# One adaLN transformer kernel: its second layer run over three turns instead of two, and its 32x32 turns moved from TensorE to VectorE and DRAM

## The chip, the cores and the metric

One Trainium2 chip, one of its cores. The metric is the device time in microseconds (us) of one execution of the whole program. The engines are TensorE (PE, with its weight loads as PEld), VectorE (DVE), ScalarE (ACT), GpSimd (POOL) and SyncE (SP), which issues most transfers. All data are float32.

## The reference, cut to what matters

Eight sequences of 512 tokens with 256 features pass through a layer 0, then through layer 1, whose attention block is itself a stack of four pre-norm blocks, then through a grouped attention with a mixture of experts. The change touches the stack of four blocks only:

```
for i in range(4):
    x = x + self_attention(layer_norm(x, ln1_g[i], ln1_b[i]), Wq[i], Wk[i], Wv[i], Wo[i], bo[i])
    h = layer_norm(x, ln2_g[i], ln2_b[i])
    x = x + (gelu(h @ W1[i] + b1[i], approximate=False) @ W2[i] + b2[i])
```

Of the 8 heads of 32 features, 4 are local: a block of 128 queries sees its own and the preceding block of keys through a masked softmax. The other 4 are linear: softmax over the features of q, elu(k) + 1, running sums of k^T v over buckets of 64 tokens. W1 is 256x1024, W2 is 1024x256.

## The kernel before, in words

The function `layer1` holds this stack. A sequence in a block is one **turn** g, and there are 4 x 8 = 32 turns, numbered 0 to 31, always in the order block by block and sequence by sequence; the residual rows of all sequences stay in the tile `y`. Each engine has its own hand-written list, and semaphores with counts that grow with g tie them together. The PE list has 33 rounds: in round g it does the attention of turn g and the MLP (`hidden`, the product with W1, then `down`, the product with W2) of turn g - 1, cut into pieces between the attention's steps. There are two PSUM banks `M[0]` and `M[1]` (6 and 7) for the MLP, two `V` banks (4 and 5) and four `S` banks (0 to 3) for attention.

A round on PE before the change: `project` (tokens' values, then q and k, L1408 and L1415), `turn` (eight 128x128 transposes of the normed rows `xn` against the identity, L1398, whose result ScalarE scales into `h2T`), `scores` (L1425), eight `hidden` products (L1435) with the linear heads' `linear_turn` (L1442), `scores` of query blocks 2 and 3 and `context` (L1449) in between, `linear_out` (L1461), then 32 `down` products (L1473) in four pieces with `probs_turn` behind each (L1489: 28 transposes of the probabilities), `values` (L1501), `out_proj` (L1516).

On the other engines, in the order of their lists: VectorE adds the attention's result to `y` (`attn_sum`, L1190), takes mean and variance (`stats`, L1137, L1140) and norms (`norm`, L1146) for the second layer norm, prepares the linear heads (L1202 to L1212), masks the scores and takes their minimum (L1222), sums the contexts (`context_sum`, L1229 to L1239), inverts the sums of exponentials (`invert`, L1245), norms the next turn's rows, copies the turned probabilities out of PSUM (`probs_out`, L1251) and adds the MLP's result (`mlp_sum`, L1197). ScalarE copies PSUM to SBUF, takes exponentials (`exps`, L1336) and Gelu (L1373), with a table load at each change of function. GpSimd takes the inverse deviation (L1070, L1071), adds the biases (L1105, L1118), scales the linear queries (L1109) and multiplies the probabilities with the inverted sums (`normalise`, L1090).

The first layer norm's rows of turns 1 to 31 already go another way, `move_turned1`: one VectorE instruction transposes `xn` in blocks of 32x32 (L1154) into `score`, SyncE writes the blocks with four transfers of 128 KB into DRAM (L1013), waits until they have landed, and reads them back as 512 KB with the features on the partitions (L1017). SyncE's list is in order: a wait in it holds back every transfer behind it. It also loads weights at a block's first and last sequences and, in 8 turns, writes 1 MB of zeros each for a later stage (L1002).

In rounds 0 to 6 and 26 to 31 VectorE and GpSimd also norm and modulate a sequence on its way into or out of the stack (`stats_x`, `modulate`, `gated`). `idle_products` are products that nobody reads; they stand where PE has no MLP to do.

## Time and profile before

| what | value |
|---|---|
| median of 3 runs | 3123.52 us (3122.75 to 3123.99) |
| the profiled execution's own time | 3120.52 us |
| its span, first to last instruction | 3118.7 us |
| mean granted TensorE clock | 0.979 |
| PE busy | 2921.5 us (94%) |
| DVE, ACT, POOL busy | 1676.6, 1415.3, 827.9 us |
| layer 1's 32 turns and the end of its MLP | from 717.85 to 2477.52 us of the span |

In the profile a line L1435 is line 1435 of the kernel. A group's row tells the engine, the line, the operation, what it writes and reads, how often, its busy time in total and the mean length of one; matmuls overlap, so that a matmul's own length is more than its share of the time. A timeline row tells start, length, engine and line of instructions in a row; in brackets stands the idle time before it and who ended it. A float32 matmul stands in the trace as two records. A row of the windows view tells the stretch, its length, then busy time and instructions of PE, PEld, DVE, ACT and POOL, the granted clock of PE (1.00 is full speed), the busy share of the transfer engines and what they moved in GB/s.

### The profile page before, as it was taken

What the parts mean: (1) busy time and instruction counts of PE and PEld (TensorE: products, weight loads), DVE (VectorE), ACT (ScalarE), POOL (GpSimd) and SP (SyncE); (2) the same over time, 40 slices, a digit from 0 to 9 for tenths busy, and PEclk for the clock granted to TensorE, in tenths of its full rate; (3) what the DMA queues carried; (4) which work ended last, traced back from release to release, by engine and by line L of the source; (5) the groups of instructions that cost most, each with busy time, mean ns of one, the idle gap of its engine ahead of it and who ended that gap; (6) DMA issues with size and microseconds to landing.
All of it is one profiled execution on the core that took longest, in us unless ns stands there. A gap on an engine that the chain in (4) does not pass through costs nothing. (4 is left out here: it accounts for less than half of the span.)

```text
span 3118.7 us, 53260 instructions
## 1 busy us (share of the span) xinstructions
PE 2921.5 (94%) x20742; PEld 1958.5 (63%) x20742; DVE 1676.6 (54%) x5013; ACT 1415.3 (45%) x3117; POOL 827.9 (27%) x829
## 2 busy tenths in 40 slices
PE   6889999888999999999999999999999788799998
PEld 3566666664666666565666666665656444468887
DVE  4677776755655545545445444456555478641112
ACT  3666666633445354444444453544444134132224
POOL 1001111113323322322323223233333310025552
PEclk8999999999999999999999999999999899899999
DMA  4111111002000112010211000110100000023325
GB/s 140 18 19 19 18 19 19 13 3 72 25 28 18 38 31 69 28 55 28 67 47 35 21 14 28 32 55 20 38 20 25 11 1 28 27 68 80 75 84 189
DMA packets 102249, 126.48 MB, mean 41 GB/s; under 512 B 12451, under 2 KB 79014, under 8 KB 100960
## 3 DMA queue, kind: packets, MB, share of 16 engines
q1 hardware_dynamic: 93168, 102.56, 11.4%
q0 software_dynamic: 7680, 16.32, 2.1%
q8 instruction: 166, 2.72, 0.4%
q10 hardware_dynamic: 1152, 4.19, 0.3%
q14 instruction: 83, 0.68, 0.1%
HBM read 75.56 MB, written 43.61 MB: 38 GB/s over the span
## 5 line engine op out<-in xcount | busy, mean ns | idle before, releaser
L1435 PE MATMUL bank<-h2T,w 128*128 128x512 f32 x1024 | 478.8, 606 | 5.2 <-ACT gT L1373 3.7
L1473 PE MATMUL bank<-w,gT 128*128 128x256 f32 x2048 | 465.9, 381 | 0.0
L1473 PEld LDWEIGHTS bank<-w,gT 128*128 128x128 f32 x2048 | 379.3, 190 | 49.7 <-issue 0.5
L1090 POOL TENSOR_TENSOR prob<-prob,rsum 128x512 f32<-128x512 f32 (+1 forms) x256 | 237.9, 950 | 592.4 <-DVE rsum L1245 592.4
L1435 PEld LDWEIGHTS bank<-h2T,w 128*128 128x128 f32 x1024 | 182.2, 190 | 223.8 <-issue 173.6
L1373 ACT ACTIVATE gT<-bank,vec 128x512 f32<-128x512 f32 x256 | 175.1, 687 | 285.5 <-PE bank L1435 284.0
L609 ACT ACTIVATE y<-y,least 128x128 f32<-128x128 f32 (+3 forms) x512 | 252.0, 554 | 50.6 <-DVE least L479 50.6
L479 DVE CUSTOM_DVE_ANT_0 y<-bank,mask 128x128 f32<-128x128 f32 (+3 forms) x512 | 223.9, 485 | 70.2 <-PE bank L706 68.9
L1222 DVE CUSTOM_DVE_ANT_0 prob<-bank,mask 128x256 f32<-128x256 f32 (+1 forms) x512 | 164.3, 387 | 168.3 <-PE bank L1425 168.3
L1336 ACT ACTIVATE prob<-prob,least 128x256 f32<-128x256 f32 (+1 forms) x512 | 239.6, 471 | 15.8 <-DVE least L1222 15.5
L1251 DVE COPY probT<-bank 128x1024 f32<-128x1024 f32 (+1 forms) x128 | 138.4, 1082 | 189.7 <-PE bank L1489 189.7
L722 PE MATMUL bank<-ident,y 128*128 128x128 f32 x1280 | 183.5, 280 | 46.3 <-DVE probT L284 33.3
L1408 PE MATMUL bank<-wtok,hT 128*128 128x512 f32 x512 | 225.0, 592 | 1.3 <-ACT hT L1327 1.3
L722 PEld LDWEIGHTS bank<-ident,y 128*128 128x128 f32 x1280 | 143.5, 142 | 110.8 <-issue 90.0
L1390 ACT COPY aoT<-bank 128x512 f32<-128x512 f32 x32 | 18.8, 586 | 366.6 <-PE bank L1501 366.6
L1354 ACT COPY tok<-bank 128x384 f32<-128x384 f32 x128 | 61.3, 479 | 234.9 <-PE bank L1408 234.9
L1408 PEld LDWEIGHTS bank<-wtok,hT 128*128 128x128 f32 x512 | 97.2, 190 | 110.2 <-issue 108.6
L2371 DVE COPY yout<-bank 128x512 f32<-128x512 f32 x40 | 27.7, 692 | 256.8 <-PE bank L2503 256.8
L284 DVE COPY probT<-bank 128x512 f32<-128x512 f32 (+1 forms) x160 | 101.2, 633 | 119.1 <-PE bank L722 119.1
L1146 DVE TENSOR_SCALAR xn<-y,mv,rstd 128x256 f32<-128x256 f32 x256 | 132.9, 581 | 52.3 <-POOL rstd L1071 52.3
L2491 PE MATMUL bank<-inT,we 128*128 128x256 f32 x640 | 144.8, 379 | 2.4 <-ACT inT L2422 2.4
L2503 PE MATMUL bank<-we,score 128*128 128x256 f32 x640 | 144.6, 379 | 0.0
(328 smaller groups left out, 5050.2 us busy)
## 6 DMA issues: line engine op xcount, KB each, us to landing
turned_rows<-score SPq DMA_DIRECT2D x124, 128.0 KB, 2.3
score<-turned_rows SPq DMA_DIRECT2D x31, 512.0 KB, 3.6
w<-in_W SPq DMA_DIRECT2D x8, 1024.0 KB, 7.6
expert_parts<-zeros SPq DMA_DIRECT2D x8, 1024.0 KB, 6.1
we<-in_we SPq DMA_DIRECT2D x16, 512.0 KB, 5.0
rows<-modulation SPq DMA_DIRECT2D x40, 128.0 KB, 3.5
x<-in_x SPq DMA_DIRECT2D x8, 512.0 KB, 6.3
prob<-score SPq DMA_DIRECT2D x64, 64.0 KB, 2.3
```

The source lines that it names most:

```text
L479: nc.vector.tensor_tensor_reduce(out=prob[:, j, FROM[tile]:FROM[tile] + width], in0=S[:, j, at:at + width], in1=mask[:, T - width:T], scal ...
L609: ins = nc.scalar.activation(one, one, ACT.Exp, bias=least[:, n % 2, tile, j:j + 1], scale=-1.0)
L722: ins = nc.tensor.transpose(H[at % 2][:, col:col + P], prob[:, j0 + j, src:src + P], c.ident[:, :])
L1090: nc.gpsimd.tensor_tensor(two, two, rsum[:, at:at + 2].unsqueeze(2).to_broadcast([P, 2, width]), ALU.mult).then_inc(s["probs"], 1)
L1222: nc.vector.tensor_tensor_reduce(out=prob[:, at, from_col(q):PAIR], in0=S[:, j, off:off + width], in1=mask[:, from_col(q):PAIR], scale=1.0 ...
L1336: nc.scalar.activation(one, one, ACT.Exp, bias=least[:, at:at + 1], scale=-1.0, accum_out=sums[:, at:at + 1]).then_inc(s["exped"], 1)
L1373: nc.scalar.activation(gT[:, m, :], M[m % 2][:, :], ACT.Gelu, bias=v[:, 4 * KD + m:4 * KD + m + 1]).then_inc(s["gelu_done"], 1)
L1408: ins = nc.tensor.matmul(S[:, t, :], hT[:, k, 1 + t * P:1 + (t + 1) * P], wtok[:, k, :], start=(k == 0), stop=(k == KD - 1))
L1435: ins = nc.tensor.matmul(M[m % 2][:, :], w1[:, k, m * P:(m + 1) * P], h2T[:, k, :], start=(k == 0), stop=(k == KD - 1))
L1473: ins = nc.tensor.matmul(M[i][:, (t % 2) * D:(t % 2 + 1) * D], gT[:, m, t * P:(t + 1) * P], w2[:, m, :], start=(m == 0), stop=(m == MF - 1))
L2491: ins = nc.tensor.matmul(UP[(2 * j + i) % 4][:, (m % 2) * CHUNK_T:(m % 2 + 1) * CHUNK_T], w1[e % 2][:, k, m * P:(m + 1) * P], inT[j % 2][: ...
L2503: ins = nc.tensor.matmul(DOWN[j % 2][:, t * D:(t + 1) * D], gT[j % 2][:, k, t * P:(t + 1) * P], w2[e % 2][:, k, :], start=(k == 0), stop=( ...
```

## The change

- The MLP of a turn is spread over two later rounds: round g does `hidden` of turn g - 1 and `down` of turn g - 2, so that there are 34 rounds. `down` now stands in the first half of a round, `hidden` in the second. `down` waits for all eight Gelus of its turn.
- `turn` for the second layer norm is gone from the rounds: `turn_rows` transposes both norms' rows in 32x32 blocks on VectorE, `move_rows1` and `move_rows2` take them through DRAM, and ScalarE's `gains_in` scales both.
- `probs_turn` and `probs_out` are gone: `turn_probs` transposes the probabilities in 32x32 blocks from `prob` to a new tile `prob_blocks` on VectorE, and `move_probs` takes them through DRAM in two halves: query blocks 0 and 1 (12 blocks of 32 columns, 768 KB), then 2 and 3 (16, 1 MB), each as four transfers out, a wait, and one back in. `values` waits for each half.
- Seven of eight `hidden` products stand ahead of `values`, one behind it (`EARLY`).
- GpSimd's bias `bo` is added earlier, and the first norm of the next turn moves to the end of VectorE's list. The zeros are written in 32 pieces of 256 KB, two in each of 16 turns.

```diff
-            for g in range(TURNS + 1):
-                mlp, attn = g > 0, g < TURNS
+            for g in range(TURNS + 2):
+                attn, down_of, hidden_of = g < TURNS, g >= 2, 1 <= g <= TURNS
                 if attn:
                     project(g)
-                if mlp:
-                    pe.wait_ge(s["norm2"], g)
-                    for half in range(KD):
-                        if g >= 2:
-                            pe.wait_ge(s["w2_added"], 2 * (g - 2) + half + 1)
-                        turn(half, "turn2_full")
+                if down_of:
+                    down(g - 2, 0, 4)
                 if attn:
                     pe.wait_ge(s["lin_out"], g + 1)
                     pe.wait_ge(s["qk_out"], 2 * (g + 1))
                     scores(g, (0, 1))
-                if mlp:
-                    pe.wait_ge(s["w1_loaded"], 16 * ((g - 1) // B + 1))
-                for m in range(MF):
-                    if mlp:
-                        hidden(g - 1, m)
-                    if attn:
-                        if m == 0:
-                            linear_turn(g)
-                        if m == 2:
-                            pe.wait_ge(s["score_min"], 16 * g + 8)
-                            scores(g, (2, 3))
-                        if m == 3:
-                            pe.wait_ge(s["lin_k_ready"], g + 1)
-                            context(g)
-                if mlp:
-                    pe.wait_ge(s["w2_loaded"], 16 * ((g - 1) // B + 1))
+                if down_of:
+                    down(g - 2, 4, 12)
+                elif attn:
+                    idle_products(c, 4, 7)
+                if attn:
+                    pe.wait_ge(s["score_min"], 16 * g + 8)
+                    scores(g, (2, 3))
+                if down_of:
+                    down(g - 2, 12, 17)
+                if attn:
+                    linear_turn(g)
+                    pe.wait_ge(s["lin_k_ready"], g + 1)
+                    context(g)
+                if down_of:
+                    down(g - 2, 17, NT * MF)
+                elif attn:
+                    idle_products(c, 4, 7)
                 if attn:
                     pe.wait_ge(s["qlT_out"], g + 1)
-                    if not mlp:
-                        idle_products(c, 7, 7)
                     linear_out(g)
-                pieces = NT * MF
-                at = 0
-                for q, upto in enumerate((10, 17, 24, pieces)):
-                    if mlp:
-                        down(g - 1, at, upto)
-                        at = upto
-                    elif q in (1, 2):
-                        idle_products(c, 1, 7)
-                    if attn:
-                        probs_turn(g, q)
+                if hidden_of:
+                    pe.wait_ge(s["w1_loaded"], 16 * ((g - 1) // B + 1))
+                    for m in range(EARLY):
+                        hidden(g - 1, m)
+                elif attn:
+                    idle_products(c, 7, 7)
                 if attn:
                     values(g)
+                if hidden_of:
+                    for m in range(EARLY, MF):
+                        hidden(g - 1, m)
+                if attn:
                     out_proj(g)
```

```diff
+            def move_probs(g, h):
+                sp.wait_ge(s["probs_turned"], 4 * g + 2 * h + 2)
+                if g:
+                    probs_in[h].wait(sp, 16 * g)
+                    sp.wait_ge(s["av_full"], g)
+                dram = c.probs_dram[h]
                 for i in range(GROUPS):
...
+                    src = pblocks[h][SQUARE * i:SQUARE * (i + 1), :, :, :].rearrange("p a k r -> p a (k r)")
+                    sp.dma_start(dram[:, :, i, :].rearrange("a p n -> p a n"), src).then_inc(probs_away[h].sem, 16)
+                probs_away[h].wait(sp, 16 * GROUPS * (g + 1))
+                sp.dma_start(probT[h].rearrange("p i k r -> p (i k r)"), dram.rearrange("a p i n -> (a p) (i n)"))\
+                  .then_inc(probs_in[h].sem, 16)
...
-            for g in range(TURNS):
+            for g in range(TURNS + 2):
...
+                if 1 <= g <= TURNS:
+                    move_rows2(g - 1)
...
+                if g < TURNS:
+                    move_probs(g, 0)
+                    move_probs(g, 1)
...
+                if g + 1 < TURNS:
+                    move_rows1(g + 1)
+                if B <= g < B + parts // 2:
+                    clear(2 * (g - B))
+                    clear(2 * (g - B) + 1)
```

```diff
                     context_sum(g)
-                    invert(g, 0)
+                    turn_probs(g, 0)
+                    invert(g, 2)
+                    turn_probs(g, 1)
+                    if g >= 2:
+                        mlp_sum(g - 2, 0)
+                    invert(g, 3)
+                    if g >= 2:
+                        mlp_sum(g - 2, 1)
+                    turn_probs(g, 2)
+                    turn_probs(g, 3)
```

The order of the instructions at the three places on which the prediction rests:

PE, from the context to the output projection of one turn in the middle of the stack, before (`h2T,w` is `hidden`, `w,gT` is `down`, `ident,prob` the probabilities' transposes, `probT,tok` is `values`, `wo,aoT` is `out_proj`):

```order
L1449 MATMUL bank<-v_linear,tok 32x33 x28
L1435 MATMUL bank<-h2T,w 128x512 x8
L1461 MATMUL bank<-qlT,ctx_normed 32x64 x28
L1473 MATMUL bank<-w,gT 128x256 x10
L1489 MATMUL bank<-ident,prob 128x128 x4
L1473 MATMUL bank<-w,gT 128x256 x7
L1489 MATMUL bank<-ident,prob 128x128 x8
L1473 MATMUL bank<-w,gT 128x256 x7
L1489 MATMUL bank<-ident,prob 128x128 x8
L1473 MATMUL bank<-w,gT 128x256 x8
L1489 MATMUL bank<-ident,prob 128x128 x8
L1501 MATMUL bank<-probT,tok 32x128 x28
```

and the same engine after the change, one whole turn from the second half of `down`'s first piece on:

```order
L1534 MATMUL bank<-w,gT 128x256 x8
L1485 MATMUL bank<-kT,qT 128x256 x8
L1534 MATMUL bank<-w,gT 128x256 x5
L1504 MATMUL bank<-ident,tok 128x128 x4
L1511 MATMUL bank<-v_linear,tok 32x33 x28
L1534 MATMUL bank<-w,gT 128x256 x15
L1523 MATMUL bank<-qlT,ctx_normed 32x64 x28
L1497 MATMUL bank<-h2T,w 128x512 x14
L1547 MATMUL bank<-probT,tok 32x128 x28
L1497 MATMUL bank<-h2T,w 128x512 x2
L1562 MATMUL bank<-wo,aoT 128x256 x8
```

The 28 transposes between the pieces of `down` are gone, `down` stands ahead of the linear heads' output, and 14 of 16 `hidden` matmuls stand between that and `values`.

VectorE, from the contexts' last instruction to the last sum of the MLP, before:

```order
L1239 TENSOR_TENSOR ctx_normed<-ctx,kcum 128x224
L1245 RECIPROCAL rsum<-sums 128x4
L1137 BN_STATS bn<-y 128x6 x4
L1140 BN_AGGR mv<-bn 128x2 x4
L1245 RECIPROCAL rsum<-sums 128x4
L1146 TENSOR_SCALAR xn<-y,mv,rstd 128x256 x4
L1154 STREAM_TRANSPOSE score<-xn 128x4x8x32
L1251 COPY probT<-bank 128x512
L1245 RECIPROCAL rsum<-sums 128x4
L1251 COPY probT<-bank 128x1024
L1197 TENSOR_TENSOR y<-y,bank 128x512
```

and after, to the transpose of the next turn's rows:

```order
L1297 TENSOR_TENSOR ctx_normed<-ctx,kcum 128x224
L1213 STREAM_TRANSPOSE prob_blocks<-prob 128x4x4x32
L1303 RECIPROCAL rsum<-sums 128x4
L1213 STREAM_TRANSPOSE prob_blocks<-prob 128x8x4x32
L1255 TENSOR_TENSOR y<-y,bank 128x512
L1303 RECIPROCAL rsum<-sums 128x4
L1255 TENSOR_TENSOR y<-y,bank 128x512
L1213 STREAM_TRANSPOSE prob_blocks<-prob 128x8x4x32 x2
L1183 BN_STATS bn<-y 128x6 x4
L1186 BN_AGGR mv<-bn 128x2 x4
L1192 TENSOR_SCALAR xn<-y,mv,rstd 128x256 x4
L1198 STREAM_TRANSPOSE score<-xn 128x4x8x32
```

The four copies of turned probabilities have become four transposes, the last two of them behind both sums of the MLP (L1255), and the norm of the next turn's rows stands behind them.

SyncE, one turn in which zeros are written, before:

```order
L1013 DMA turned_rows<-score 32x8x128 x4
L1017 DMA score<-turned_rows 128x2x512
L1002 DMA expert_parts<-zeros 128x2048
```

and after:

```order
L1028 DMA turned_rows<-score 32x8x128 x4
L1030 DMA score<-turned_rows 128x2x512
L1057 DMA turned_probs<-prob_blocks 32x4x384 x4
L1059 DMA probT<-turned_probs 128x1536
L1057 DMA turned_probs<-prob_blocks 32x4x512 x4
L1059 DMA probT<-turned_probs 128x2048
L1028 DMA turned_rows<-score 32x8x128 x4
L1030 DMA score<-turned_rows 128x2x512
L1020 DMA expert_parts<-zeros 128x512 x2
```

Five transfers of a turn have become twenty, in one queue: second norm, first half of the probabilities, second half, first norm of the next turn.

## Rows read from the trace of the kernel before

**Rows 1.** The windows view: turn 0, turns 2 to 25, turns 26 to 31, the end, one stretch

```profile
717.85:761.97 44.12, 37.42 (x291) 20.78 (x292) 25.61 (x83) 15.19 (x46) 13.46 (x14) 0.88 0.11 32
815.57:2100.31 1284.74, 1279.54 (x9025) 819.39 (x9024) 652.82 (x2048) 590.44 (x1392) 392.92 (x371) 1.00 0.12 36
2100.31:2429.47 329.16, 321.19 (x2257) 204.17 (x2255) 187.08 (x581) 145.58 (x346) 116.20 (x106) 1.00 0.08 24
2429.47:2477.52 48.05, 30.77 (x105) 20.08 (x104) 17.84 (x49) 8.34 (x11) 9.37 (x9) 0.85 0.00 0
752.70:756.10 3.40, 3.12 (x13) 2.15 (x12) 1.22 (x1) 0.00 (x0) 2.30 (x3) 0.51 0.45 115
```

**Rows 2.** The timeline of PE in the turn that starts at 1511.67 us

```profile
1521.97 1.04 PE L1398 MATMUL bank<-ident,xn 128*128 128x128 f32 x8
1522.94 0.94 PE L1425 MATMUL bank<-kT,qT 32*128 32x128 f32 x16
...
1534.27 7.13 PE L1435 MATMUL bank<-h2T,w 128*128 128x512 f32 x16
1541.33 0.98 PE L1461 MATMUL bank<-qlT,ctx_normed 32*32 32x64 f32 x56
...
1546.66 0.60 PE L1489 MATMUL bank<-ident,prob 128*128 128x128 f32 x4
1547.10 3.19 PE L1473 MATMUL bank<-w,gT 128*128 128x256 f32 x14
```

**Rows 3.** The timeline of DVE in the same turn

```profile
1515.96 1.38 DVE L1146 TENSOR_SCALAR xn<-y,mv,rstd 128x256 f32<-128x256 f32 x4 [1.54 <-POOL rstd L1071]
...
1548.49 1.25 DVE L1154 STREAM_TRANSPOSE score<-xn 128x1024 f32<-128x1024 f32 x1
...
1552.34 0.68 DVE L1197 TENSOR_TENSOR y<-y,bank 128x512 f32<-128x512 f32 x1
```

**Rows 4.** Groups of instructions by line over the whole span, for ACT, POOL and PE

```profile
L1336 ACT ACTIVATE prob<-prob,least 128x256 f32<-128x256 f32 (+1 forms) x512 | 239.6, 471 | 15.8 <-DVE least L1222 15.5
L1090 POOL TENSOR_TENSOR prob<-prob,rsum 128x512 f32<-128x512 f32 (+1 forms) x256 | 237.9, 950 | 592.4 <-DVE rsum L1245 592.4
L1343 ACT ACTIVATE hT<-score,vec 128x512 f32<-128x512 f32 x62 | 47.2, 813 | 0.0
L1516 PE MATMUL bank<-wo,aoT 128*128 128x256 f32 x512 | 127.6, 392 | 2.4
L1501 PE MATMUL bank<-probT,tok 128*32 128x128 f32 x1792 | 62.2, 276 | 2.8
```

**Rows 5.** The timeline of the transfers' issues on SP, two turns

```profile
1549.77 1.84 SPq L1013 DMA_DIRECT2D turned_rows<-score  x4
1553.47 0.38 SPq L1017 DMA_DIRECT2D score<-turned_rows  x1
...
1335.71 1.84 SPq L1013 DMA_DIRECT2D turned_rows<-score  x4
1341.27 0.38 SPq L1017 DMA_DIRECT2D score<-turned_rows  x1
```

**Rows 6.** The page's DMA issues: KB each, median us from issue to landing

```profile
score<-turned_rows SPq DMA_DIRECT2D x31, 512.0 KB, 3.6
w<-in_W SPq DMA_DIRECT2D x8, 1024.0 KB, 7.6
expert_parts<-zeros SPq DMA_DIRECT2D x8, 1024.0 KB, 6.1
```

**Rows 7.** The timeline of PE: an idle gap in turn 0, then the end of the stack

```profile
752.16 0.63 PE L1489 MATMUL bank<-ident,prob 128*128 128x128 f32 x4 [2.42 <-POOL prob L1090]
...
2435.12 1.97 PE L1398 MATMUL bank<-ident,xn 128*128 128x128 f32 x8 [5.49 <-DVE xn L1146]
2437.19 14.83 PE L1435 MATMUL bank<-h2T,w 128*128 128x512 f32 x32
2451.86 13.98 PE L1473 MATMUL bank<-w,gT 128*128 128x256 f32 x64
```

284 lines of the change are left out of this document (147 added, 137 removed).

## The prediction, on record before the changed kernel ran

> **What bounds the kernel now.** I read the windows view first. Turns 2 to 25 take 1284.74 us, so 53.53 us each, PE is busy for 1279.54 us of that, and the granted clock is 1.00 [rows 1]. In this stretch nothing but PE's own work counts: a microsecond taken from PE's list is won, one taken from another engine is not, until that engine becomes late. Turns 26 to 31 take 54.86 us each (329.16 / 6), because VectorE also serves sequences that leave the stack. Turn 0 (44.12 us) and the end behind the last output projection (48.05 us) are the places where PE waits, with clocks of 0.88 and 0.85. VectorE is busy for half of a middle turn (652.82 of 1284.74 us), ScalarE for 46%. So the question is twofold: how much PE work goes, and does anything that replaces it arrive later than PE gets there?
>
> **What goes from PE.** The timeline of one turn [rows 2] gives each piece from start to start. The eight transposes of the normed rows take 1521.97 to 1522.94, 0.97 us. Four transposes of probabilities take 1546.66 to 1547.10, 0.44 us, so the 28 of a turn 3.08 us. Together 4.05 us of 53.53; nothing of them was hidden, since PE has no gaps. The other products are the same in number and shape; only their place changes. The turned probabilities that `values` now reads lie in runs of 32 floats, not in one of 128; no row shows such a read on PE, and I take it at nothing (upper bound: as much as `values` itself again, 62.2 / 32 = 1.9 us a turn [rows 4]). A middle turn becomes **49.5 us**.
>
> **What is added, and its cover.** VectorE: four copies out of PSUM go, four transposes of the same sizes come, which by the existing transpose cost 1.25 us each and half for the narrow one [rows 3], together 4.4 us. One more transpose of rows, 1.25 us, is new. Even with nothing taken off for the copies VectorE has 27.2 + 5.6 = 33 us of work in 49.5, so its total is no issue, its order is. ScalarE scales `h2T` from SBUF instead of PSUM, the same two instructions. GpSimd does the same work in another order.
>
> The transfers are what can be late. The row pattern is known: four writes of 128 KB are issued at 1549.77, landed by 1553.47 (3.70 us for 512 KB), and the read back of 512 KB lands 3.6 us later [rows 5, 6]. The worst write set before took 5.56 us (1335.71 to 1341.27) [rows 5].
>
> For the second half of the probabilities, 1 MB each way, the rows give bounds. A read of 512 KB takes 3.6 us; 1 MB of zeros, issued 0.4 us behind such a read, takes 6.1 us [rows 6]. So 1.5 MB land in about 6.5 us: 2.9 us for each added MB, and 5.0 us for 1 MB alone. The write set gets 3.70 + 0.5 x 2.9 = 5.15 us as long as its pieces are no more efficient; they are 2 KB long instead of 512 bytes, so I take 4.5. Sum **9.5 us**, between 8.7 (what two 512 KB legs and 0.7 us a leg give) and 12.6 (5.56 and a weight-like read of 7 us).
>
> **Does it arrive?** PE has, from the end of `down` to the second half of `values`: `linear_out` 0.9 us (1541.33 on), seven `hidden` products at 7.07 / 4 = 1.77 us [rows 2], 12.4 us, and the first 12 of 28 products of `values`, 0.8 us: 14.1 us. VectorE, from the same moment: the second sum of the MLP, 0.7 us, two transposes, 2.5 us [rows 3], so 3.3 us with the hand-overs. That leaves **10.8 us** for 9.5 us of transfers: it arrives with about 1.3 us to spare. The probabilities of the last query block must be scaled by then. On ScalarE they stand behind the copy of `qlT` (0.6), one set of four exponentials (4 x 0.47 = 1.9), the two gains (2 x 0.81) and the last set (1.9), 6.0 us from the end of `linear_turn` [rows 4]; then GpSimd needs 2 x 0.95 = 1.9 us. PE fills the same time with the context and 15 `down` products at 13.98 / 32 = 0.44 us [rows 7], 6.6 us and more. So they are ready a good microsecond after `down` ends at the latest, before the 2 us at which VectorE asks for them. The first half starts 5 us earlier and is no issue.
>
> The second norm's rows: attention's sums, statistics and norm end 5.6 us into the turn (at the end of the stack the same chain takes 2429.47 to 2435.12 [rows 1, 7]), the transpose 1.25 and two legs 7.3 bring them in at 14.3 us. ScalarE asks for them after some 22 us and PE at 29 us: hidden. The next turn's rows: on VectorE statistics, inverse deviation and norm (that 5.6 us without the sum, 4.7) and a transpose, 1.25, behind the 3.3 us, then 7.3 us of transfers and 1.6 us of gains, 18 us after `down` ends; PE's next `project` comes after 0.9 + 8 x 1.77 + 1.9 + 4.0 = 21 us [rows 4]. Hidden with 3 us in hand, and SyncE, where they stand behind the second half's write set only (its read is issued, not awaited), is free by then. The weight loads of the three block changes share the engines with a read; at 1 us each they cost 3 us at most, and I leave them in the range.
>
> In ten of the turns 2 to 31 VectorE has 5 us more to do (`stats_x`, `modulate`), now ahead of `context_sum`. It had some 4 us of slack there, so the last transposes come up to a microsecond later and eat the 1.3 us. Such turns cost between nothing and the 1.35 us that the last six show now (54.86 - 53.51). I take 0.5 us, 5 us in all.
>
> **Head.** Turn 0 has no cover: its last probabilities are ready near 31 us (now 35, with the norm of the next rows ahead of them), then transpose and legs 9.5, the last part of `values` 1.2, a copy 0.6, `out_proj` 4.0: 47 us, and a slow stretch of clock, 1 us: 48. Turn 1 loses its `down` (14 us of PE work) and is bound by the same chain: 47. Together 95 for 97.7 now: -3 us.
>
> **End.** Now: norm at 5.65, `hidden` 14.83, `down` 13.98 [rows 7], and 11.7 us to the next stage (2465.8 to 2477.5): 48.05. After: `down` of turn 30 runs first, 14 us; the sums that free its banks stand on VectorE behind a sequence's `stats_x` and `modulate` and end near 19 us (the rows through DRAM are in at 16 us); `hidden` 15, the last Gelu 0.8, `down` 14, then 11.7: 60.5. **+12.5 us.** The pipeline's extra depth costs no more than this, since the `down` of turn 30 is work that turn 31 no longer does.
>
> **Sum.** Turns 2 to 31: now 1284.74 + 329.16 = 1613.9 us; after 30 x 49.48 + 5 = 1489.4: -124.5. Head -3, end +12.5: **-115 us**. The profiled execution took 3120.5 us, its span 3118.7, so it becomes 3005.5. The median of the runs shown is 3.0 us above it: **3008 us**.
>
> **The page's rule against it.** What the rows show is that two small legs through DRAM cost 7.3 us for 512 KB that a strided pattern cuts into runs of 512 bytes [rows 5, 6]. The Trainium skill, page "VectorE: DVE Perf Modes", section "The three transpose paths", warns that a plain DMA copy that transposes by its access pattern is 19 times slower than the DMA's own transpose, and section "Rules for kernel authors" leaves a 128x128 transpose to TensorE. By that the legs would take over 80 us a turn and the kernel about double. Here VectorE turns within the blocks and the transfer moves only whole runs, so the trace speaks against its applying.
>
> **Rivals.** (A) *The second half comes 1 to 3 us late in every turn.* For it: the window is 10.8 us and its upper bound 12.6; reads of half one overlap the writes of half two; 5.56 us for a write set has been seen. Against: most write sets take 3.7 us, and a middle turn's transfers (5.6 MB) are little for engines that move at over 200 GB/s in a stretch. At 1.9 us (the excess of the slow write set) in 30 turns it costs 57 us: 3065 us; at 3 us 3098.
>
> (B) *The wait at `values` cools the clock, and the kernel is slower.* In turn 0 PE waited 2.42 us ahead of 752.16 [rows 7], and the stretch from 752.70 on ran at a granted clock of 0.51 [rows 1]. If the legs take 13.5 us, PE waits 2.7 us in each turn, and the following 3.4 to 6.8 us run at half speed, 1.7 to 3.4 us lost. Wait plus clock are then 4.4 to 6.1 us, more than the 4.05 won. At 6.1: 30 x 6.1 = 183, 3191 us; at 4.4 3140. It decides from about 2.4 us of wait on, that is legs of 13.2 us. Against it: 13.2 is beyond both upper bounds. The Trainium skill, page "TensorE: Matmul & The Clock Gate", section "HAM oscillation", describes this: a loop that waits for a transfer in each pass begins each pass slow.
>
> (C) *VectorE is the late one*: `hidden` may not begin before the MLP's first sum, which stands behind `context_sum`, two transposes and an inversion. With 5 us more in ten turns it may come a microsecond late: 10 us, 3018 us. Inside my range.
>
> **Chances.** Forecast with C: 0.70 (own range 2982 to 3035; the low end has no waits and 0.4 us less of gaps a turn for the fewer changes between kinds of products). A: 0.23. B, with the page's rule: 0.06. Gains and waits that cancel: 0.01. The range takes A up to 3070. A measurement of this kernel tells 0.2% (6 us) from no change. Faster 0.93, same 0.01, slower 0.06.
>
> **What would show it.** Turn starts at a distance of 49.5 us in the middle; no idle time ahead of `values` (L1547); clock 1.00 through the turns; the second half's read landing 9 to 10 us after the last transpose of probabilities; turn 0 and turn 1 near 48 us; `down` of turn 31 ending some 13 us later behind its output projection. Wrong it is if PE idles more than 1 us at L1547 or L1497 in middle turns, if `values` takes longer than 2 us, or if the clock falls there.

## The result: 3198 us, slower by 2.4%

The changed kernel takes 3198.12 us (median of 4 runs, 3195.74 to 3198.97); the kernel before takes 3123.2 us beside it. The ratio is 1.0238, with a 95% interval of 1.0221 to 1.0256. The forecast was 3008 us, with a range that ended at 3070. The time lies 7 us beyond the upper end of what rival B gave, 3140 to 3191.

The windows view of the profiled execution after (its span is 3195.3 us) answers to [rows 1]: turns 0 and 1, turns 2 to 6, turns 7 to 25, turns 26 to 31, the end of the stack. The columns are the window and its length, then busy time and count of PE, PEld, DVE, ACT and POOL, the granted clock of PE, DMA share and GB/s.

```profile
716.58:829.11 112.53, 88.66 (x566) 45.94 (x567) 58.88 (x180) 38.81 (x103) 28.79 (x31) 0.85 0.34 99
829.11:1115.77 286.66, 256.81 (x1701) 158.89 (x1700) 170.74 (x495) 123.56 (x290) 86.78 (x85) 0.95 0.38 107
1115.77:2141.40 1025.63, 956.07 (x6461) 589.56 (x6460) 521.50 (x1586) 471.16 (x1102) 301.45 (x287) 0.97 0.43 126
2141.40:2492.48 351.08, 310.39 (x2040) 191.83 (x2041) 206.93 (x561) 147.82 (x346) 113.77 (x101) 0.94 0.35 102
2492.48:2554.03 61.55, 43.86 (x162) 30.82 (x160) 26.73 (x70) 7.01 (x10) 14.45 (x13) 0.88 0.09 24
```

Where the time came from, against before: turns 2 to 31 take 286.66 + 1025.63 + 351.08 = 1663.4 us where they took 1613.9, so +49.5; turns 0 and 1 112.5 where they took 97.7, +14.8; the end 61.55 for 48.05, +13.5. With 1.3 us less ahead of the stack and 0.1 more behind it, this is the 76.6 us between the spans. A turn of 7 to 25 is 1025.63 / 19 = **54.0 us**; it was 53.5, and 49.5 was forecast. PE idles 69.6 us there (3.7 a turn; 47.7 us of it at `values`, 17.9 at `project`), and its clock is not 1.00.

The page's groups (busy, mean ns | idle time before them, and what ended it) name the wait; they answer to [rows 4]:

```profile
L1137 POOL TENSOR_TENSOR prob<-prob,rsum 128x512 f32<-128x512 f32 (+1 forms) x256 | 236.0, 949 | 147.8 <-DVE rsum L1303 147.8
L1468 PE MATMUL bank<-wtok,hT 128*128 128x512 f32 x512 | 235.4, 614 | 23.6 <-ACT hT L1397 22.4
L1391 ACT ACTIVATE prob<-prob,least 128x256 f32<-128x256 f32 (+1 forms) x512 | 239.3, 470 | 14.0 <-DVE least L1280 14.0
L1547 PE MATMUL bank<-probT,tok 128*32 128x128 f32 x1792 | 76.7, 320 | 116.9 <-DMA probT<-turned_probs 116.9
```

`values` (L1547) waits 116.9 us for the turned probabilities, where it waited 2.8 before [rows 4]. `project` (L1468) waits 22.4 us for the next turn's rows. The timeline of PE in a middle turn, and the end of the turn before it, with the wait in brackets:

```profile
1485.56 3.62 PE L1562 MATMUL bank<-wo,aoT 128*128 128x256 f32 x16
1491.63 8.64 PE L1468 MATMUL bank<-wtok,hT 128*128 128x512 f32 x16 [2.45 <-ACT hT L1397]
...
1521.80 0.98 PE L1523 MATMUL bank<-qlT,ctx_normed 32*32 32x64 f32 x56
1522.72 12.28 PE L1497 MATMUL bank<-h2T,w 128*128 128x512 f32 x28
1534.93 0.86 PE L1547 MATMUL bank<-probT,tok 128*32 128x128 f32 x24
1538.01 1.08 PE L1547 MATMUL bank<-probT,tok 128*32 128x128 f32 x32 [2.21 <-DMA probT<-turned_probs]
```

The first 12 of the 28 products of `values` (24 records) run at once, the other 16 (32 records) wait 2.21 us. The issues on SP in the same turn: four writes of the first half, its read, four writes of the second half, its read, then the next turn's rows:

```profile
1519.42 2.15 SPq L1057 DMA_DIRECT2D turned_probs<-prob_blocks  x4
1524.26 0.34 SPq L1059 DMA_DIRECT2D probT<-turned_probs  x1
1524.97 3.39 SPq L1057 DMA_DIRECT2D turned_probs<-prob_blocks  x4
1531.86 0.34 SPq L1059 DMA_DIRECT2D probT<-turned_probs  x1
1532.31 2.56 SPq L1028 DMA_DIRECT2D turned_rows<-score  x4
1539.57 0.38 SPq L1030 DMA_DIRECT2D score<-turned_rows  x1
```

The second half's write set takes 1524.97 to 1531.86, 6.9 us (7.1 in the median turn), and the page gives 6.1 us for its read; the forecast had 4.5 and 5.0. **The legs are 13.2 us in place of 9.5.** The rows behind them need 7.3 us for 512 KB that took 3.70 before [rows 5]. The page's DMA issues (KB each, median us to landing):

```profile
turned_probs<-prob_blocks SPq DMA_DIRECT2D x128, 256.0 KB, 5.4
probT<-turned_probs SPq DMA_DIRECT2D x32, 1024.0 KB, 6.1
turned_rows<-score SPq DMA_DIRECT2D x252, 128.0 KB, 2.4
score<-turned_rows SPq DMA_DIRECT2D x63, 512.0 KB, 3.8
turned_probs<-prob_blocks SPq DMA_DIRECT2D x128, 192.0 KB, 3.1
probT<-turned_probs SPq DMA_DIRECT2D x32, 768.0 KB, 4.9
```

### The profile page after: what moved, and what is told of

It reads as the page before. It is cut to its first block and busy times, and to the rows that moved or that the text cites. A ratio compares the mean times of both kernels' runs of the same rounds, so it can differ in the third digit from the quotient of the medians.

```text
span 3195.3 us, 51547 instructions
## 1 busy us (share of the span) xinstructions
PE 2854.1 (89%) x19618; PEld 1875.6 (59%) x19618; DVE 1747.0 (55%) x5045; ACT 1419.7 (44%) x3115; POOL 824.9 (26%) x829
## 5 line engine op out<-in xcount | busy, mean ns | idle before, releaser
L1497 PE MATMUL bank<-h2T,w 128*128 128x512 f32 x1024 | 490.1, 634 | 10.5 <-issue 5.4
L1534 PE MATMUL bank<-w,gT 128*128 128x256 f32 x2048 | 474.2, 385 | 0.9 <-ACT gT L1445 0.9
L1497 PEld LDWEIGHTS bank<-h2T,w 128*128 128x128 f32 x1024 | 200.1, 201 | 250.8 <-issue 248.7
L1248 DVE TENSOR_TENSOR y<-y,bank 128x512 f32<-128x512 f32 x64 | 44.0, 687 | 492.1 <-PE bank L1562 492.1
L1468 PE MATMUL bank<-wtok,hT 128*128 128x512 f32 x512 | 235.4, 614 | 23.6 <-ACT hT L1397 22.4
L1117 POOL TENSOR_SCALAR ve<-mv 128x4 f32<-128x4 f32 x64 | 14.6, 229 | 814.6 <-DVE mv L1186 814.6
L1468 PEld LDWEIGHTS bank<-wtok,hT 128*128 128x128 f32 x512 | 99.7, 197 | 142.6 <-issue 141.7
L1547 PE MATMUL bank<-probT,tok 128*32 128x128 f32 x1792 | 76.7, 320 | 116.9 <-DMA probT<-turned_probs 116.9
```

The source lines that it names most:

```text
L1468: ins = nc.tensor.matmul(S[:, t, :], hT[:, k, 1 + t * P:1 + (t + 1) * P], wtok[:, k, :], start=(k == 0), stop=(k == KD - 1))
L1497: ins = nc.tensor.matmul(M[m % 2][:, :], w1[:, k, m * P:(m + 1) * P], h2T[:, k, :], start=(k == 0), stop=(k == KD - 1))
L1534: ins = nc.tensor.matmul(M[i][:, (t % 2) * D:(t % 2 + 1) * D], gT[:, m, t * P:(t + 1) * P], w2[:, m, :], start=(m == 0), stop=(m == MF - 1))
```

## The experiments

Each is the changed kernel with the edit shown, run beside the kernel before; ratios are against that kernel, with 95% intervals. Experiment 1 was run once, 2 to 5 twice, 6 ten times, 7 and 8 four times. The kernel before took between 3123.2 and 3132.3 us in the different series, so differences of a few us between series mean nothing.

### 1. No transfers of probabilities

This kernel leaves the probabilities' transfers out and multiplies with zeros, so it shows the change without its legs.

```diff
-                if g < TURNS:
-                    move_probs(g, 0)
-                    move_probs(g, 1)
...
-                    if q % 2 == 0:
-                        probs_in[q // 2].wait(pe, 16 * (g + 1))
```

> Leaves out all transfers of the probabilities and every wait on them; values reads a tile that was set to zero once, so the local heads' result is zero. Theory L (the second half of the probabilities lands some 3 us late, and the wait also cools the clock): middle turns 49.5 us, clock 1.00 through the turns, no idle time at L1547, the turns with modulate near 50 us; about 2980 to 2995 us in all. Rival P (the pipeline itself is dearer than I counted: values reads runs of 32, the pieces of down and hidden lie badly, VectorE is late): middle turns stay above 52 us with idle time at hidden or values, 3100 us or more.

Measured: 3012.8 us, 18 us above the range of theory L and far from its rival; 10 us of that lie ahead of the stack, which begins at 727.1 us of the span and not at 716.6. Its windows of turns 7 to 25 and 26 to 31, in the same columns:

```profile
1073.48:1999.47 925.99, 924.97 (x6461) 580.26 (x6460) 531.11 (x1577) 469.58 (x1102) 300.14 (x285) 1.00 0.23 64
1999.47:2307.43 307.96, 294.48 (x2042) 184.37 (x2041) 210.37 (x570) 147.98 (x346) 114.99 (x103) 0.99 0.16 45
```

A middle turn takes 925.99 / 19 = 48.7 us at clock 1.00 with 0.05 us of idle time. So what PE saves is real, and the whole loss hangs on the transfers. Set beside after it also splits the 5.2 us a turn: idle time 69.6 - 1.0 = 68.5 us, 3.6 a turn, and PE's busy time 956.07 - 924.97 = 31.1 us, 1.6 a turn, which is nearly all the same work done at a lower clock.

### 2. What makes the second half late: VectorE, size, or order?

Second half's first transpose ahead of the MLP's second sum; first half filled up to 1 MB; first half's read behind the second half's writes:

```diff
+                    turn_probs(g, 2)
                     if g >= 2:
                         mlp_sum(g - 2, 1)
-                    turn_probs(g, 2)
```

```diff
-PROBS = (12, 16)
+PROBS = (16, 16)
```

```diff
-                probs_away[h].wait(sp, 16 * GROUPS * (g + 1))
...
                     move_probs(g, 0)
                     move_probs(g, 1)
+                    read_probs(g, 0)
+                    read_probs(g, 1)
```

> VectorE transposes the third query block's probabilities ahead of the MLP's second sum, in the time in which it waits for the end of down. Theory L: the second half's first write goes out 1.2 us earlier in the middle turns (30.5 us into the turn instead of 31.7), the wait at the second part of values falls from 2.4 to 1.2 us there, with fewer slow stretches of clock; nothing in the turns with modulate, where VectorE never waits; 25 to 45 us faster than the changed kernel. Rival P, or a wait that is set by something else than VectorE: within 5 us of it.

> The first half gets 16 blocks instead of 12 (four of them never used), so that its writes are pieces of 2048 bytes instead of 1536, with a third more bytes. If the 1536-byte pieces are what holds the queue: the first half's write set takes about 3.9 us instead of 4.85, its read overlaps less with the second half's writes, and these take 6.2 us instead of 7.1; 20 to 30 us faster than the changed kernel. If the engines are bound by bytes: the second half's legs take as long or longer, no gain or up to 20 us slower.

> The first half's read is issued behind the second half's writes instead of ahead of them. If the read of the first half is what stretches the second half's write set from 4.5 to 7.1 us: that set lands in 4.5 to 5 us, and both reads then share the way back, second part of values 1 to 2 us earlier, 20 to 50 us faster than the changed kernel. If 1 MB simply takes that long to DRAM: the write set stays near 7 us and the reads come later, up to 60 us slower.

Measured: 3206.29 us (1.0239, 1.0191 to 1.0288), 3275.26 us (1.046, 1.0406 to 1.0513) and 3187.58 us (1.018, 1.013 to 1.0229).

The first shows that VectorE hardly sets the start. SP had issued the second half's writes at 31.7 us of a turn and issued them at 31.5 now: until 31.1 it stands in its list at the wait for the first half's write set. Nothing was won where 25 to 45 us were forecast.

The second gives the law of a write set. The first half's, with nothing else of the probabilities in flight, takes 4.86 us for 768 KB (median of turns 7 to 25) and, filled up, 6.1 us for 1 MB in 9 of these 19 turns (median 6.35, longest 7.9); rows of 512 KB take 3.70 [rows 5]. That is 3.70, 4.86, 6.1, so 1.2 us for each 256 KB more, some 220 GB/s. The three lie on one line though their pieces are 512, 1536 and 2048 bytes long, so no discount for longer pieces shows. The same run has the second half's set at 8.5 us, beside a first half's read of 1 MB, where it takes 7.1 beside one of 768 KB: the read beside it lengthens it.

The third does not take the first half's read out of the way; it only moves it. SP's issues, eight writes and two reads:

```profile
1506.88 8.39 SPq L1063 DMA_DIRECT2D turned_probs<-prob_blocks  x8
1515.31 4.63 SPq L1052 DMA_DIRECT2D probT<-turned_probs  x2
```

The first read goes out when the eighth write has been issued, and still has more than 4 us of the second half's write set beside it, which lands just before the second read is issued. The set keeps its 7.2 us, and turns 7 to 25 take 54.2 us, no less than 54.0. The 10 us that the kernel is faster come from turns 0 to 6, which take 15 us less, and the interval of its ratio meets that of the changed kernel (1.0221 to 1.0256), so even they are not sure.

### 3. The wait and the clock

Five idle products of 512 columns ahead of the second part of `values`:

```diff
                 for q in range(4):
+                    if q == 2:
+                        idle_products(c, 5, 1)
                     if q % 2 == 0:
```

> Five products that nobody reads (2.2 us at full clock) stand ahead of the second part of values, in the time in which PE waits anyway. If the slow clock behind the wait is a cost of its own: the clock stays at 1.00 in the middle turns, these fall from 54.2 to near 52 us, and the kernel is 25 to 45 us faster than the changed one. If not: the same within 10 us, or slower by up to 1 us a turn.

Measured: 3178.63 us (1.0168, 1.0148 to 1.0189). PE in a middle turn:

```profile
1316.07 0.86 PE L1549 MATMUL bank<-probT,tok 128*32 128x128 f32 x24
1316.86 4.56 PE L107 MATMUL bank<-y,ident 128*128 128x512 f32 x10
1321.35 1.08 PE L1549 MATMUL bank<-probT,tok 128*32 128x128 f32 x32
```

The five products take 4.5 us, twice the wait that they cover and twice the 2.2 us that were expected, and the kernel is still 20 us faster. In turns 7 to 25 what they cost and what they win cancel: these take 1023.6 us for 1025.6. PE is busy for 1015.1 us of that, less 86.6 us of idle products 928.5, so of the 31.1 us that the lower clock cost all but 3.5 are back. The rest of the 20 us lies in turns 2 to 6 (278.3 for 286.7) and 26 to 30 (282.8 for 292.0).

The clock itself says which waits do it. In turns 7 to 25 of the changed kernel the granted clock falls 15 times to its lower level, 1.2 GHz, for 65 us in all: 11 times behind a wait at `values` (of 2.2 to 3.9 us), 4 times behind one at `project` (of 2.5 to 5.9 us). Half of PE's busy time in these stretches is 21 us behind `values` and 8 behind `project`. Eight other waits at `values`, of 1.4 to 2.6 us, were not followed by one, and with the idle products one of the 15 is left. So waits of some 2.2 us do cost clock, though not each of them, as rival B had it. The Trainium skill, page "TensorE: Matmul & The Clock Gate", section "HAM oscillation", describes a loop that waits for a transfer in each pass and begins the next pass slow; this trace agrees for 11 of the 19 turns, with waits of 2.2 to 3.9 us.

### 4. Why a write set is slow: issue time or partitions?

ScalarE, the other engine with a queue of its own, issues half of the writes. In the first version SyncE has partitions 0 to 63 and ScalarE 64 to 127; in the second they have 0-31 and 64-95, and 32-63 and 96-127; the third keeps one queue and changes only the order:

```diff
-                for i in range(GROUPS):
-                    src = pblocks[h][SQUARE * i:SQUARE * (i + 1), :, :, :].rearrange("p a k r -> p a (k r)")
-                    sp.dma_start(dram[:, :, i, :].rearrange("a p n -> p a n"), src).then_inc(probs_away[h].sem, 16)
+                probs_out(sp, h, (0, 1))
...
+                probs_out(nc.scalar, h, (2, 3))
```

```diff
-                probs_out(sp, h, (0, 1))
+                probs_out(sp, h, (0, 2))
...
-                probs_out(nc.scalar, h, (2, 3))
+                probs_out(nc.scalar, h, (1, 3))
```

```diff
-                for i in range(GROUPS):
+                for i in (0, 2, 1, 3):
```

> The changed kernel, but two of each half's four writes (partitions 64 to 127) are issued by ScalarE on its own queue, at the same time as SyncE's two (partitions 0 to 63). Theory W (a write set moves at some 200 GB/s because its transfers, each out of 32 partitions, stand one behind the other in one queue): both write sets become shorter, the first from 4.85 to about 3.4 us, the second from 7.1 to under 5, the second part of values waits for 0 to 1 us in middle turns (51 us a turn or less); 60 to 100 us faster than the changed kernel. Rival D (DRAM takes writes at that rate, or the engines are full): write sets unchanged, time within 15 us of the changed kernel.

> The two-queue version of the changed kernel with the groups of 32 partitions dealt out otherwise: SyncE writes partitions 0-31 and 64-95, ScalarE 32-63 and 96-127 (before: SyncE 0-63, ScalarE 64-127). Theory (two queues help because the two halves of the partitions, 0-63 and 64-127, are read from SBUF side by side, each over ports of its own): now both queues begin with a group of the same half, the first half's write set takes 4.8 us again instead of 4.1, the second's 7 instead of 5.9, in all 3180 to 3195 us. Rival (two queues help because the issues no longer stand one behind another): sets of 4.1 and 5.9 us as before, 3150 to 3165 us.

> The changed kernel with one queue, as it is, but the four groups of 32 partitions written in the order 0-31, 64-95, 32-63, 96-127. Theory (ports): neighbouring writes in the queue read from different ports and overlap, so the first half's write set takes 4.1 to 4.4 us instead of 4.85 and the second's 6 to 6.5 instead of 7.1, in all 3155 to 3180 us. Rival (issue time on one queue): nothing changes, 3185 to 3200 us.

SP's issues of the first half in a middle turn of the first version, the second and the third, each in a fence of its own:

```profile
1552.07 0.80 SPq L978 DMA_DIRECT2D turned_probs<-prob_blocks  x2
1556.14 0.34 SPq L1063 DMA_DIRECT2D probT<-turned_probs  x1
```

```profile
1518.24 0.78 SPq L978 DMA_DIRECT2D turned_probs<-prob_blocks  x2
1523.12 0.34 SPq L1063 DMA_DIRECT2D probT<-turned_probs  x1
```

```profile
1562.18 1.96 SPq L1057 DMA_DIRECT2D turned_probs<-prob_blocks  x4
1566.48 0.34 SPq L1059 DMA_DIRECT2D probT<-turned_probs  x1
```

| kernel | queues | write sets, median of turns 7 to 25 | time | ratio |
|---|---|---|---|---|
| changed | SP: 0, 1, 2, 3 | 4.86 and 7.06 us | 3198.12 | 1.0238 (1.0221 to 1.0256) |
| first version | SP: 0, 1; ACT: 2, 3 | 4.07 and 6.10 us | 3158.45 | 1.0104 (1.0084 to 1.0124) |
| second version | SP: 0, 2; ACT: 1, 3 | 4.89 and 7.23 us | 3206.03 | 1.0245 (1.0207 to 1.0283) |
| third version | SP: 0, 2, 1, 3 | 4.30 and 6.71 us | 3181.16 | 1.0166 (1.0132 to 1.0199) |

Issue time is not the cause. Two queues that both begin with a group of the lower 64 partitions win nothing, though each issues only two transfers; one queue in alternating order wins a good part of what two queues with the right groups win. The first version gave less than its theory had (sets of 3.4 and under 5 us, 60 to 100 us; it was 40 us). In the other two the sets came out as forecast (the second half's 0.2 us above in both), the times 11 and 1 us above the ranges. So what counts is which groups are neighbours: groups of the same half of the partitions follow one another, groups of the two halves overlap. One thing is not separated: a group of partitions always goes to the same place in DRAM, so that a new order also changes which places are neighbours there. No run changes the one without the other. For the partitions speaks the rate. The Trainium skill, page "SBUF — State Buffer", section "Door 1: The DMA port swizzle", says that partitions 0 to 31 and 0 to 63 reach the same 8 of 16 ports and gives 189 GB/s for 1 MB from 32 partitions; the 220 GB/s above, which leave out the fixed part, agree with the 218 GB/s that it gives as the limit for 8 ports. The same page's section "Can I just issue two DMAs to hit both halves?" answers no, with a gain of 6%. Here the first half's set went from 4.86 to 4.07 us, 16% less, so this trace speaks against that "no".

### 5. VectorE's order in the turns with `modulate`

`modulate` behind the last transposes, and the bias `bo` behind the linear heads' q on GpSimd, as before the change (the lines of `bo` are not shown):

```diff
-                    if g + 1 < B:
-                        modulate(g + 1)
-                    if last >= 0:
-                        modulate(B + last)
                     context_sum(g)
...
                     turn_probs(g, 3)
+                    if g + 1 < B:
+                        modulate(g + 1)
```

> modulate stands behind the last transposes of probabilities instead of ahead of context_sum, and GpSimd adds the bias bo where it did before the change, so that it no longer runs beside VectorE's linear_in. The middle turns 7 to 25 should not change. If VectorE's extra work in the other turns is what makes them 57 to 60 us: the first write of the second half goes out near 31.7 us into those turns instead of 34.7 and 37.2, they fall to 54 or 55 us, 40 to 50 us in all. Rival: they are bound by the rows of the next turn (or by the clock), and gain less than 10 us.

Measured: 3176.07 us (1.016, 1.0109 to 1.0211). Turn 0 takes 51.7 us (56.3 in the changed kernel), turns 2 to 6 54.0 to 55.5 (55.9 to 58.3), turns 27 to 30 54.5 to 56.8 (58.5 to 60.2); the middle stays near 54 (54.4). The last transposes of probabilities end at 31.7 us of turns 2 to 6 and 32.4 of turns 27 to 30, where they ended at 33.6 and 36.2. So the turns fell nearly as forecast, but the kernel gained 22 us and not 40 to 50, and its two runs lie 26 us apart. The two edits were not tried singly.

### 6. Putting them together

First two queues, the order of experiment 5 and the early transpose of experiment 2:

> The two queues, the earlier third transpose, modulate and bo as in the run before, all together. Theory W: second half issued near 30.5 us into a turn, landed before PE gets there at 42.5; turns of 48.7 to 49.5 us, clock 1.00; 3020 to 3050 us in all, faster than the kernel before the change by 2 to 3%. Rival D: above 3130 us.

Measured: 3126.53 us (0.9995, 0.9982 to 1.0009), the time of before: not the theory's 3020 to 3050, and just below its rival's 3130. The second half's writes went out at 31.1 us of a turn, 0.7 earlier, but its set took 7.4 us where it took 6.1 with two queues alone, and the wait at `values` stayed at 1.9 us. Then, without the early transpose, with four idle products; with all eight `hidden` ahead of `values` (`EARLY = MF`); and with both:

> The changed kernel with two queues for the writes, the bias added later on GpSimd, modulate behind the last transposes, and four idle products of 512 columns ahead of the second part of values. Theory (the remaining cost is the wait of 1.0 to 1.3 us and the half clock that follows it in some turns): middle turns uniformly 51.0 to 51.5 us, clock 1.00, in all 3085 to 3105 us. Rival (ScalarE's later issue costs what it wins, as in the combination before): 3120 to 3130 us.

> The same without idle products, but with all eight hidden products of the MLP ahead of the product with the values, where the change has seven: the window of the second half grows by 1.77 us to 12.5 us, and two queues need some 11.5. Theory (window against legs decides): no wait at the second part of values in middle turns, clock 1.00, a copy of 0.6 us exposed ahead of the output projection: middle turns at 49.3 to 50.0 us, in all 3040 to 3070 us. Rival (the legs grow with the window, because other transfers or ScalarE's place in its list set them): middle turns stay at 50.4 to 53 us, 3090 to 3120 us.

> As the one before, with two idle products of 512 columns ahead of the second part of values. If nothing is waited for any more, they cost their own 0.4 us in each turn: 12 us more than without them. If a wait of a few tenths is left that they cover, the same time, with a steadier clock: within 5 us.

Measured: 3122.41 us (0.9986, 0.9972 to 1.0), 3125.54 us (1.0006, 0.9995 to 1.0018) and 3115.33 us (0.996, 0.9943 to 0.9976). The first is the time of its rival, the second lies above both cases, and the third, expected within 5 us of the second or 12 above it, is 10 below. In the second, with the window wider by 1.77 us, the wait at `values` is down to 6.3 us in the 19 middle turns together, 0.3 a turn, but they still take 53.7 us each. SP, ACT and PE at the end of one (of 52.2 us) show why, in this order:

```profile
1543.68 2.62 SPq L1034 DMA_DIRECT2D turned_rows<-score  x4
1550.88 0.38 SPq L1036 DMA_DIRECT2D score<-turned_rows  x1
...
1555.30 1.52 ACT L1401 ACTIVATE hT<-score,vec 128x512 f32<-128x512 f32 x2 [4.18 <-DMA score<-turned_rows]
...
1556.97 3.88 PE L1484 MATMUL bank<-wtok,hT 128*128 128x512 f32 x5 [2.50 <-ACT hT L1401]
```

Beside the second half's read the write set of the next turn's rows takes 7.2 us, and PE waits 2.50 us for them at `project`, 76.6 us in the 32 turns. The wait had only moved.

### 7. The next turn's rows out of the way

From turn 7 on the next turn's norm and transpose stand behind the linear heads' shift, where VectorE waits for PE anyway, and their transfers ahead of the probabilities':

```diff
+                if ahead:
+                    stats(nxt, "stats1")
                 if g < TURNS:
                     linear_in(g)
+                    if ahead:
+                        norm(nxt, "rstd1", g + 2, "norm1")
+                        turn_rows("norm1", g + 2)
...
+                    write_rows1(g + 1)
...
+                    read_rows1(g + 1)
                     move_probs(g, 0)
```

> The changed kernel with one thing moved: from turn 7 on, the next turn's statistics stand ahead of the linear attention's shift on VectorE, its norm and transpose right behind it (where VectorE waits for PE anyway), its rows are written to DRAM right behind the other rows and read back ahead of the probabilities, so that nothing but the probabilities moves in the second half of a turn. Theory (the second half's legs are long because other transfers share the queue and the time): second half's write set 6 us instead of 7.1, wait at the second part of values about 1.2 us, middle turns 51.0 to 51.5 us, 3120 to 3145 us. Rival (the legs are their own length, the rows never disturbed them): the wait stays at 2.2 us, middle turns at 54 us, 3185 to 3200 us.

> The same move together with two queues for the writes, the bias later on GpSimd, modulate behind the last transposes, and all eight hidden products ahead of the values. In the run without this move, PE waited 2.6 us a turn at the projection for the next rows, whose write set took 7.2 us beside the read of the probabilities. Theory (that wait is the rest of the loss): no wait at the values nor at the projection from turn 7 on, middle turns at 49.3 to 50 us, clock 1.00, in all 3050 to 3080 us. Rival (another wait takes its place, VectorE's transposes in the first part of the turn make the scores late): middle turns 51 us and more, 3100 us and more.

Measured on the changed kernel alone: 3225.53 us (1.0314, 1.0293 to 1.0335), slower. The first half's write set now shares its time with the rows' read and takes 5.7 us, so the second half starts and lands later. Theory and rival both missed: the rows had not disturbed the second half, and moved there they disturb the first. VectorE's norm also meets GpSimd's addition of `bo`; the same instruction twice, and GpSimd beside the second:

```profile
1552.51 1.38 DVE L1210 TENSOR_SCALAR xn<-y,mv,rstd 128x256 f32<-128x256 f32 x4 [1.55 <-POOL rstd L1134]
...
1558.72 3.18 DVE L1210 TENSOR_SCALAR xn<-y,mv,rstd 128x256 f32<-128x256 f32 x4
...
1558.36 2.44 POOL L1176 TENSOR_TENSOR y<-y,bo 128x1024 f32<-128x1024 f32 x1
```

Together with two queues, the wide window, `bo` and `modulate` later, the same move is the last piece: **3046.77 us (0.9741, 0.972 to 0.9761)**. Its windows of turns 7 to 25 and 26 to 31:

```profile
1078.29:2022.31 944.02, 932.49 (x6460) 578.12 (x6461) 495.74 (x1573) 469.11 (x1102) 303.51 (x285) 1.00 0.46 137
2022.31:2340.97 318.66, 300.82 (x2042) 186.33 (x2041) 196.40 (x570) 147.38 (x346) 111.62 (x103) 0.98 0.37 113
```

49.7 us a middle turn at clock 1.00, with 0.6 us of idle time; the kernel is 3 us below the range that was expected. That this is nearly the 49.5 us of the prediction is in part luck: PE's work is 0.8 us shorter than forecast (experiment 1), while 0.6 us of waits come on top and `out_proj`, which in the wider window stands right behind `values`, takes 0.4 us more from start to start. Turns 27 to 30, whose VectorE also serves a sequence that leaves, still take 54.3 to 55.5 us. This version beats both kernels, the one before by 2.6%. The wide window was not run without the two queues, so that its share is not known.

### 8. The other part alone

Probabilities turned by PE and copied by VectorE as before; the three-turn order and the rows of both norms through DRAM stay (PE's transposes of blocks 0 and 1 between the last pieces of `down`, of 2 and 3 behind the second and the fourth `hidden`):

> One part of the change alone: the schedule of three turns and the rows of both norms through DRAM stay, the probabilities are turned by PE and copied out by VectorE as before the change. PE's list is then 0.97 us a turn shorter than before the change (eight transposes of rows), 52.6 us in a middle turn, and no transfer is waited for at the attention product with the values. Theory (only the legs of the probabilities spoil the change): middle turns at 52.6 to 52.8 us, granted clock 1.00 there, 30 x 0.9 = 27 us won in the stack, 12.5 us lost at its end, 3105 to 3115 us in all, so faster than before. Rival (the three-turn order itself makes VectorE or GpSimd late in the turns that carry modulate): middle turns as said, but the first seven and the last five at 55 us and more, 3120 to 3135 us, so no gain.

> Probabilities turned by PE as before the change, three-turn order and both norms' rows through DRAM kept, with the same move of the next rows (in the first try PE waited 5 us a turn at the projection, since their norm stood behind the last copies of probabilities). Theory: middle turns at 52.6 us, no waits, 3100 to 3120 us, so the order of three turns with the rows alone is worth a little, and the probabilities through DRAM another 3 us a turn where their legs are hidden. Rival (PE still waits for copies out of PSUM ahead of the values): middle turns over 53.5 us, 3130 us and more.

Measured: 3276.62 us (1.0485, 1.046 to 1.0511) and, with experiments 5 and 7's order, 3157.85 us (1.0094, 1.0074 to 1.0114). The first missed altogether; the second has its rival's time, but not for the rival's reason. In the first PE waits 4.8 us in each turn for the next rows, whose norm stands behind the last copies. In the second the window of turns 7 to 25 is

```profile
1133.29:2117.52 984.23, 984.23 (x6993) 636.03 (x6994) 496.92 (x1561) 469.20 (x1102) 301.15 (x283) 1.00 0.22 61
```

with no idle time: 51.7 us for each turn from 8 to 26, 1.8 less than before, though only 0.97 us of transposes left PE. But turns 2 to 6 take 61.4 to 62.5 us, since their rows still come last, and turns 27 to 30 58.0. Against these 51.7, turning the probabilities through DRAM is worth 2 us more a turn where its legs are hidden (49.7), and costs 2.3 where they are not (54.0).

## Why the prediction was wrong

- **What goes from PE: right.** 49.5 us were forecast for a turn without waits; it takes 48.7 (experiment 1). The reads of `values` in runs of 32 floats, taken at nothing, cost nothing: 0.86 us for 12 products and 1.08 for 16, together 1.94, as before (62.2 / 32) [rows 4]. The other 0.8 us come from the new places of the same products: from start to start `hidden` takes 0.6 us less a turn than before, `out_proj` 0.4 and `values` 0.3 less, `down` 0.5 more. The range's low end had 0.4 us for fewer changes between kinds of products; that reason does not hold, since the second kernel of experiment 8 changes kinds as often as before (24 times a turn, 23 before) and has the same 0.8 us.
- **The legs: the step that failed.** "So I take 4.5" for the write set was 7.1, "5.0 us" for the read 6.1. The write set went wrong in three terms. The prediction scaled 3.70 us up by 2.9 us for each MB, a slope read from a read and from zeros, which go over all 128 partitions; write sets out of groups of 32 cost 1.2 us for each 256 KB, 4.8 for each MB, so that 1 MB by itself takes 6.1 us and not 5.15 (experiment 2). It took 0.65 us off for pieces of 2 KB, and no such gain shows. And it put the first half's read beside the set at nothing: some 1 us more makes the 7.1, and a read of 1 MB made it 8.5. The upper bound was wrong too: 12.6 came from a 512 KB set at its worst, when the set to be bounded was 1 MB. Scaled from 3.70 us with no discount, 2 x 3.70 + 7 = 14.4 would have been the end to keep, and with 13.2 inside it rival B could not have had 0.06.
- **Does it arrive: the window was right.** 10.8 us were forecast; from SP's issue at 31.8 us of a turn to the second part of `values`, which PE reaches at 42.6, it is 10.8 (medians of turns 7 to 25). The wait follows, 13.2 - 10.8 = 2.4; it is 2.4 in the median and 1.4 to 3.9 over the 19 turns.
- **Rival B: right in its point and in its place.** It was to decide from 2.4 us of wait, or legs of 13.2 us, and it did. Its price was 4.4 to 6.1 us a turn for wait and clock; 3.6 and 1.6, together 5.2, were measured, 0.9 us of the idle time at `project`. What brings the result 7 us beyond it are the head and the turns with `modulate`, below. Its chance of 0.06 was the error.
- **SyncE "is free by then": wrong.** The rows were to be ready 9.3 us after `down`, at about 37.7 us of a turn, and without the probabilities' transfers they are issued then; but the longer write set, awaited ahead of its read, holds SP, and they went out at 39.4 (1532.31 in the turn shown), beside that read. They took 7.3 us for the 3.70 assumed, and were late (22.4 us in all, and 76.6 once the wait at `values` was nearly gone).
- **Head, forecast 95 us for turns 0 and 1, took 112.5.** The chain was right, its prices were not: the longer legs, and `modulate` and `bo` ahead of the probabilities, worth 4.6 us in turn 0 together (experiment 5), which the forecast had not put on this chain. The last transposes end at 34.4 us of turn 0, and at 30.1 with the two moved. Even without the legs the two turns take 100.5 us.
- **Turns with `modulate`, forecast at 0.5 us extra each**, take 2 to 4 us more than a middle one in turns 2 to 6 and 4.5 to 6 more in turns 27 to 30; without legs the latter still take 50.3 to 52.8 us for 48.7. The forecast had the last transposes up to 1 us later there; they end 1.9 us later in turns 2 to 6 and 4.5 us later in turns 27 to 30 (33.6 and 36.2 us of a turn, 31.7 in the middle). Part of it is that VectorE's own steps became longer beside GpSimd, where `bo` is now added earlier: the shift of the linear heads takes 0.69 us in each turn before and up to 2.68 in experiment 1, in nearly all middle turns too, which have the time for it; in turns 27 to 30 the next step takes 2.57 us for 0.42 as well. This term was mis-sized: VectorE's durations had been read from the kernel before. How much is `modulate` and how much `bo` is not separated.
- **End, +12.5 forecast, +13.5 measured.** The `down` of turn 30 runs first, `hidden` waits 5.1 us for VectorE, as described:

```profile
2492.48 13.98 PE L1534 MATMUL bank<-w,gT 128*128 128x256 f32 x64
2511.56 15.83 PE L1497 MATMUL bank<-h2T,w 128*128 128x512 f32 x32 [5.10 <-DVE y L1255]
2528.26 14.05 PE L1534 MATMUL bank<-w,gT 128*128 128x256 f32 x64 [0.87 <-ACT gT L1445]
```

- **The warning of the Trainium skill, page "VectorE: DVE Perf Modes", section "The three transpose paths"** (a plain DMA copy that transposes by its strides is many times slower) did not apply, as the prediction said: the longest of a middle turn's legs shown above takes 7.3 us, and no pair of them comes near 80.

What stays open: why the second half's write set takes 6.1 us in the two-queue version but about 7 in the combined ones. The first half's read is issued later there (30.6 to 31.2 us of a turn, 30.4 with two queues alone), nearer to it, but no run tests that by itself. Whether neighbours collide in the partitions or in DRAM is argued, not shown (experiment 4). Why only some waits of 2.2 to 2.6 us are followed by the lower clock is open too.

## What to carry to other kernels

Where a product is traded for a trip through DRAM, the window must be set against legs that are scaled up from the same pattern, in bytes and in partitions, with no discount for pieces, and the end of the range must be the scaled worst one. Order transfers so that neighbours in a queue, or the two queues, read different halves of the partitions, and look at what an in-order queue does behind each wait: whatever stands there starts late and then collides. A wait that is shortened moves to the next thing in line, so read the waits again after each step; edits that alone gave 40 us, 22 us or a loss of 27 us gave 151 together, with the wider window.

## What the runs showed of the hardware

- Write sets from groups of 32 partitions: 3.70, 4.86 and 6.1 us for 512 KB, 768 KB and 1 MB in one queue with no read of probabilities beside them, 7.1 for 1 MB beside a read of 768 KB and 8.5 beside one of 1 MB; 4.07 for 768 KB when the two halves of the partitions go side by side in two queues, 4.30 in one queue in alternating order, 4.89 with two queues on the same half.
- A read of 1 MB back into 128 partitions took 6.1 us in the median, of 768 KB 4.9.
- VectorE beside a GpSimd addition of 128x1024: a norm of 1.38 us took 3.18, a shift of 0.69 us 2.68. The Trainium skill, page "SBUF — State Buffer", section "Who interferes with whom", has the two engines share a pair of ports that one of them holds for a whole instruction; the added 1.8 and 2.0 us are close to the 2.44 us of one addition.
- With waits of some 2.4 us at `values` in each turn, and others at `project`, the granted clock fell to its lower level 15 times in 19 turns, and PE's work took 31 us more; with the 0.6 us a turn of the fastest version it kept 1.00.
